# A four-graph pipelined graph network on one core: waits that name one graph, one order text for body, first and last group, and loads issued in the order's own turn

## What is computed

```
x = LN(x + (adj @ (x W + b)) / rowsum(adj))                       # layer 0
x = LN(x + softmax_i(q_i . (adj @ (k*mask))_i / 16) * (x Wv))     # layer 1, softmax over the nodes
x = LN(x + Wo(softmax(q k^T * 32^-0.5 * (adj + adj)) v) + bo)     # layer 2, 8 heads of 32
h = relu(D^-1 H B^-1 H^T (x W1^T) + b1);  h = LN(h)*gamma+beta    # layer 3, H = (adj != 0), 512 wide
x = LN(x + D^-1 H B^-1 H^T (h W2^T) + b2)
```

## Time and profile before

| | |
|---|---|
| median of 3 runs | 2016.6 us (2013.47 to 2019.37) |
| profiled execution, first to last instruction (span) | 2020.7 us |
| busy share PE / DVE / ACT / POOL | 94% / 85% / 72% / 62% |
| mean granted TensorE clock | 0.942 |
| HBM traffic | 46 MB, 23 GB/s on average |

### The profile page before, as it was taken

The page is one execution under the profiler, slowest core; times in us unless marked ns, Lnnn a source line. Parts: engine busy times, 40 slices in busy tenths (PEclk is TensorE's granted clock), DMA queues, the critical chain, the costliest instruction groups (busy, mean ns, idle before and its releaser), DMA issues.

```text
span 2020.7 us, 53237 instructions
## 1 busy us (share of the span) xinstructions
PE 1901.2 (94%) x15357; PEld 1690.6 (84%) x15357; DVE 1708.2 (85%) x4867; ACT 1456.1 (72%) x4431; POOL 1253.2 (62%) x2568
## 2 busy tenths in 40 slices
...
DMA packets 57546, 46.14 MB, mean 23 GB/s; under 512 B 5168, under 2 KB 56880, under 8 KB 57520
## 3 DMA queue, kind: packets, MB, share of 16 engines
...
## 4 chain that ended last, share of the span: by engine, by line
PE 73%; DVE 14%; issue 6%; ACT 5%; DVEq 1%; SPq 0%; DMA 0%; ACTq 0%; POOL 0%; POOLq 0%
PE ps L390 43%; PE ps L493 6%; PE ps L461 5%; DVE hb L872 3%; PE ps L482 3%; PE ps L406 3%; PE ps L453 3%; DVE z L894 3%; PE ps L469 3%; PE ps L442 2%; ACT z L629 2%; PE ps L374 2%; PE ps L427 1%; PE ps L400 1%; ACT x L573 1%
## 5 line engine op out<-in xcount | busy, mean ns | idle before, releaser
L629 ACT ACTIVATE z<-z,z_max 128x128 f32<-128x128 f32 x1024 | 401.5, 405 | 99.1 <-DVE z_max L905 99.0
L721 POOL TENSOR_TENSOR ln_rs<-ln_ve,minus_half 128x1 f32<-128x1 f32 x640 | 364.2, 569 | 50.1
L742 POOL TENSOR_TENSOR z<-z,z_rcp 128x1024 f32<-128x1024 f32 x128 | 242.7, 1896 | 226.3 <-DVE z_rcp L912 223.4
L719 POOL TENSOR_TENSOR ln_ve<-ln_mv,eps_col 128x1 f32<-128x1 f32 x640 | 128.4, 201 | 329.4 <-DVE ln_mv L791 329.1
L724 POOL TENSOR_SCALAR ln_nm<-ln_mv,ln_rs 128x1 f32<-128x1 f32 x640 | 170.7, 267 | 112.6 <-POOL ln_rs L721 112.6
L453 PE MATMUL ps<-kT,qT 32*128 32x128 f32 x2048 | 183.5, 323 | 57.7 <-DVE axT L801 29.8
L453 PEld LDWEIGHTS ps<-kT,qT 32*128 32x128 f32 x2048 | 137.0, 207 | 99.1 <-DVE axT L801 35.6
L894 DVE SCALAR_TENSOR_TENSOR z<-ps,a_hold 128x256 f32<-128x256 f32 x512 | 191.1, 416 | 34.1 <-PE ps L461 24.2
L390 PE MATMUL ps<-w2T,mnT 128*128 128x256 f32 x1536 | 208.6, 285 | 0.8 <-DVE mnT L801 0.7
L390 PE MATMUL ps<-w1T,txT 128*128 128x512 f32 x768 | 206.8, 404 | 0.1
L629 ACT ACTIVATION_READ_ACCUMULATOR z<-z,z_max 128x1 f32 x1024 | 206.6, 202 | 0.0
...
## 6 DMA issues: line engine op xcount, KB each, us to landing
x_in<-in_x_dram SPq DMA_DIRECT2D x32, 512.0 KB, 3.4
out_dram<-y_out SPq DMA_DIRECT2D x128, 128.0 KB, 1.7
a_in<-in_adj_dram SPq DMA_DIRECT2D x31, 256.0 KB, 2.7
x<-in_L_gnn_Wqk_dram ACTq DMA_DIRECT2D x1, 512.0 KB, 5.6
h<-in_L_gnn_W_dram SPq DMA_DIRECT2D x1, 512.0 KB, 5.2
h<-in_L_gnn_W_dram ACTq DMA_DIRECT2D x1, 512.0 KB, 10.6
v<-in_L_gnn_Wo_dram SPq DMA_DIRECT2D x1, 256.0 KB, 6.3
b_all<-in_L_gnn_b_dram SPq DMA_DIRECT2D x2, 128.0 KB, 8.3
```

The source lines that it names most:

```text
L629: m = act.activation(z[:, g % 2, h, :], z[:, g % 2, h, :], ACT.Exp, bias=z_max[:, g % 2, h:h + 1], accum_out=z_sum[:, g % 2, h:h + 1])
L719: pool.tensor_tensor(ve[n][:, g:g + 1], mv[n][:, g, 1:2], eps_col[:, :], ALU.add).then_inc(eps_made[n], 1)
L721: pool.tensor_tensor(rs[n][:, g:g + 1], ve[n][:, g:g + 1], minus_half[:, :], ALU.pow).then_inc(root_made[n], 1)
L742: pool.tensor_tensor(zg, zg, z_rcp[:, g % 2, :].unsqueeze(2).to_broadcast([P, HEADS, P]), ALU.mult)\
```

## The change

1. One text per engine, `ORDER_TEXT`, with `+` on the steps that are done for the next group and, on TensorE, the bank after a colon. `FIRST` and `LAST` are no longer written out: they are the steps with and without `+`, in the body's order and with the body's banks. The order and the banks of the body are the same as before.
2. Waits that free a buffer say which graph: `before(q, g, G)` in place of `q * G`, and `before(q, g, 2)` in place of `earlier(q, g, 2)`.
3. The waits on banks name the product that owned the bank (`bank_turns`), one wait for each owner.
4. Three waits are new: `am` on `made["amx"]`, and `dinv` on `read["h1"]` and `read["y"]`.
5. SP has a text as well: `lx.0+ la.0+ store.0 store.1 store.2 store.3`, walked like the others. The first `a_in` is now loaded by SP and not by ScalarE's queue.

```
-FIRST_TEXT = {
...
-LAST_TEXT = {
...
+    "sp": """
+        lx.0+ la.0+ store.0 store.1 store.2 store.3
+    """,
+FIRST = {engine: [s for s in schedule if s[2] == 1] for engine, schedule in ORDER.items()}
+LAST = {engine: [s for s in schedule if s[2] == 0] for engine, schedule in ORDER.items()}
...
-        def earlier(q, g, depth):
-            return q * G + (g - depth + 1) if g >= depth else q * G
+        def before(q, g, depth):
+            return q * G + (g + 1 - depth)
...
-            load_x(0)
-            load_x(1)
-            load_a(1)
-            with sp.Fori(0, NG - 2) as it:
-                load_x(it + 2)
-                load_a(it + 2)
-                store(it)
-            store(NG - 2)
-            store(NG - 1)
+            walk(FIRST["sp"], -1)
+            walk(ORDER["sp"], 0)
+            with sp.Fori(1, NG - 1) as it:
+                walk(ORDER["sp"], it)
+            walk(LAST["sp"], NG - 1)
...
             def walk(schedule, it, previous):
-                first, before = place_banks(schedule, previous)
...
+                for (stage, g, ahead, b), owners in zip(schedule, bank_turns(schedule, previous)):
+                    for other, og, away in owners:
+                        q = it + away
+                        pe.wait_ge(read[other], q + 1 if other in per_group else nth(q, og))
...
             def free1(q, g):
-                after(act, made["x1t"], q * G)
-                after(act, made["amx"], q * G)
-                after(act, norm_made["ln1"], q * G)
+                after(act, made["x1t"], before(q, g, G))
+                after(act, made["amx"], before(q, g, G))
+                after(act, norm_made["ln1"], before(q, g, G))
...
-            act.dma_start(a_in[:, :, :], adj_d[0:G].rearrange("g n m -> n g m")).then_inc(a_loaded, 16)
...
             def am(q, g, o):
                 dve.wait_ge(read["at"], nth(q, g))
                 dve.wait_ge(mask_made, q + 1)
+                after(dve, made["amx"], before(q, g, G))
...
             def dinv(q, g, o):
                 dve.wait_ge(read["mp"], nth(q, G - 1))
                 after(dve, x3c_made, q * G)
+                after(dve, read["h1"], q * G)
+                after(dve, read["y"], q * G)
```

More of the change, by code:

```diff
@@ L42 @@
     "pe": """
[L43 to L47, removed]
+        at.0+:0 sc1.0:1 ax.0+:3 at.1+:4 at.2+:5 sc0.0:6 ax.1+:0 sc1.1:1 sc0.1:3 at.3+:5 h0.0+:6 h0.1+:7
@@ new lines @@
+        ax.2+:0 mp.0:1 sc0.2:2 mp.1:4 mp.2:5 pt.0:6 h0.2+:0 ax.3+:1 mp.3:2 cx.0:3 sc1.2:4 pt.1:6 wo.0:0
+        x1t.0+:1 sc1.3:2 sc0.3:4 x1t.1+:6 cx.1:7 amx.0+:0 amx.1+:1 h0.3+:2 wo.1:3 tx.0:4 xg.0+:5 x1t.2+:6
+        xg.1+:7 amx.2+:0 pt.2:1 h1.0:3 x1t.3+:4 xg.2+:5 cx.2:6 tx.1:7 amx.3+:0 xg.3+:1 wo.2:2 pt.3:3 wt.0+:5
+        h1.1:6 cx.3:7 v1.0+:0 v1.1+:1 pb.0+:2 wo.3:3 tx.2:4 v1.2+:5 mn.0:6 h1.2:7 v1.3+:0 mn.1:1 x2t.0+:2
+        tx.3:3 y.0:4 h1.3:5 x2t.1+:6 y.1:7 mn.2:0 v2.0+:1 x2t.2+:2 v2.1+:3 x2t.3+:4 y.2:5 mn.3:6 k0.0+:7
@@ L48 @@
+        k1.0+:0 y.3:1 q1.0+:2 q0.0+:3 v2.2+:4 v2.3+:5
     """,
     "act": """
[L50 to L53, removed]
@@ L56 @@
+        relu.2 x2t.0+ tx.3 mn.1 ln1_norm.1+ ln3_norm.2 relu.3 x2t.1+ ln1_norm.2+ mn.2 ln1_norm.3+ x2t.2+
+        v2.0+ v2.1+ ln3_norm.3 x2t.3+ mn.3 ln4_norm.0 k0.0+ k1.0+ ln4_norm.1 q1.0+ ln4_norm.2 q0.0+ v2.2+
+        ln4_norm.3 v2.3+
     """,
     "dve": """
-        hyper.0 asum.0 sc1.0 zmax1.0 sc0.0 ax_lo.0 zmax0.0 sc1.1 ax_lo.1 zmax1.1 h0.0 zrcp.0 sc0.1 am.0 zmax0.1
-        ln0_stats.0 h0.1 ln0_aggr.0 am.1 ax_lo.2 am.2 ln0_stats.1 zrcp.1 sc0.2 zmax0.2 h0.2 ln0_aggr.1 ln0_stats.2
-        ax_lo.3 cx_lo.0 sc1.2 ln0_aggr.2 zmax1.2 wo.0 am.3 ln2_stats.0 sc1.3 x1t_lo.0 ln2_aggr.0 zmax1.3 sc0.3
@@ L61 @@
[L61 to L65, removed]
@@ L69 @@
     "pool": """
[L70 to L73, removed]
-    """,
-}
-FIRST_TEXT = {
[L78 to L97, removed]
@@ L128, with steps, bank_turns @@
 SPLIT = ("ax", "x1t", "x2t", "cx", "tx", "mn")
[L131 to L159, removed]
+def steps(text):
+    schedule = []
+    for word in text.split():
+        word, _, bank = word.partition(":")
+        stage, g = word.rstrip("+").split(".")
+        schedule.append((stage, int(g), 1 if word.endswith("+") else 0, int(bank) if bank else None))
+    return schedule
+ORDER = {engine: steps(text) for engine, text in ORDER_TEXT.items()}
+FIRST = {engine: [s for s in schedule if s[2] == 1] for engine, schedule in ORDER.items()}
+LAST = {engine: [s for s in schedule if s[2] == 0] for engine, schedule in ORDER.items()}
+BANK = {(stage, g): bank for stage, g, _, bank in ORDER["pe"]}
+def bank_turns(schedule, previous):
+    owner, turns = {}, []
+    for stage, g, ahead, bank in previous:
+        for b in range(bank, bank + BANKS[stage]):
+            owner[b] = (stage, g, ahead - 1)
+    for stage, g, ahead, bank in schedule:
+        mine = range(bank, bank + BANKS[stage])
+        turns.append(sorted({owner[b] for b in mine if b in owner}))
+        for b in mine:
+            owner[b] = (stage, g, ahead)
+    return turns
 def build(nc, ins, out):
@@ L336, in load_a, with store, walk @@
                 sp.dma_start(a_in[:, :, :], adj_d[bass.ds(q * G, G)].rearrange("g n m -> n g m")).then_inc(a_loaded, 16)
[L338 to L342 removed]
+            def store(q, g):
+                sp.wait_ge(norm_made["ln4"], nth(q, g))
+                sp.dma_start(out[bass.ds(q * G + g, 1)].rearrange("g n d -> n (g d)"),
+                             y_out[:, g, :]).then_inc(out_stored[g], 16)
+            stages = {"lx": load_x, "la": load_a, "store": store}
+            def walk(schedule, it):
+                for stage, g, ahead, _ in schedule:
+                    stages[stage](it + ahead, g)
             with nc.allow_non_contiguous_dma(reason="vectors, once"):
```

184 lines of the change are left out of this document (82 added, 102 removed).

## The result

The changed kernel takes 2179.0 us (median of 4 runs, 2177.6 to 2181.2) against 2015.0 us for the kernel before in the same comparison: a ratio of 1.082, 95% interval 1.080 to 1.084. It is 8% slower, 164 us by the medians and 156.8 us between the two profiled executions (2177.5 and 2020.7 us). The forecast was 2161 us, the range 2095 to 2222.

The account below looks back on a forecast made before the run. TensorE (PE), busy 94% of the span, was taken to bound the kernel. Seams 117 + clock 21 + registers 3 + first group 1 + last group 2 = 144 us on 2016.6 gave 2161 us, range 2095 to 2222.

Parts of the forecast that it names:

- SP's order costs, at 30 seams: Between turns, loads now issued behind the previous group's stores make everything 3.9 us later per seam, 117 us in all.
- The landing: At the seam, a_in lands at 927.5, 0.7 to 1.0 us after x_in; PE stands still 5.7 us before at.0.
- DVE's wait for a_in: Before the mask copy at each seam, DVE idles some 3 us in a wait that a DMA ends.
- The line of the Trainium skill: Fixed 2.0 us plus bytes over 436 GB/s: both loads in at 927.0, shift 3.4 us, sum 15 us less; not used.
- The shift behind the load and the clock: Per turn, 3.9 us later from the late load, plus 0.7 us for the lower clock (21 us in all).
- The clock's price: TensorE at its lower clock level: 6.8 us more there cost 2.7 us, so 0.4 us each.
- Narrower waits free nothing early: In the body, waits naming one graph are met long before they are asked: 0 us, bounds 0 and -19.
- Register work, 0.1 us per turn, 3 us: 6 more instructions each on ACT, DVE and POOL per turn, one or two on the seam's path; may be 0 or 7.
- First and last group, 1 + 2 us: Outside the turns, derived orders cost +1 us first (bounds -1, +4) and +2 us last (bounds -3, +8).
- the loads did not stay hidden: Rival: a_in lands before DVE comes to a_sum, so the seam costs nothing; 2004 to 2023 us, chance 0.03.
- the first rival: At the seam the load lands as if alone and the clock gives nothing: 2.7 us each, 2104 us, chance 0.14.
- The second: Rival: each standstill costs one more 6.8 us piece at the lower clock, 6.7 us per seam; 2221 us, chance 0.13.

Follow-up runs that it names:

- experiment 1: The changed kernel with SP's order alone undone, loads of group it+2 again ahead of the stores of group it: 2028.9 us, ratio 1.007.
- experiment 2: The kernel before with SP's order alone, loads of group it+1 behind the stores of group it-1: 2166.6 us, ratio 1.075.
- experiment 12: The kernel before with one wait more: POOL starts xb.0 at the head of a turn only when DVE's hyper.0 is done: 1919.6 us, ratio 0.954.
- experiment 4: The changed kernel with 21 matmuls of no use on PE ahead of at.0 in the loop: 2130.7 us, ratio 1.058.
- experiment 7: The kernel of experiment 1 with the buffer waits back on the previous group: 2010.3 us, ratio 0.996.
- experiment 6: The kernel before with only the derived first and last group, banks dealt as before: 2029.0 us, ratio 1.007.
- experiment 3: The changed kernel with SP's load of a_in ahead of that of x_in: 2147.2 us, ratio 1.066.

## Why the prediction was right

Step by step:

- *SP's order costs, at 30 seams.* Right, by experiments 1 and 2, one undoing it and one doing it alone: 150 and 150 us.
- *The landing.* Predicted: a_in in at 927.5 with ln4_norm.3 ending at 922.12, 5.4 us; measured 995.18 - 989.83 = 5.35 us. That it is so close is luck, since two errors of 0.4 us cancel. The loop's turn of SP took 0.58 us (990.33 to 990.91) where 0.2 was allowed. And the forecast counted the 3.4 us to x_in's landing from the end of its issue, where the page counts them from its start: 990.91 + 3.5 = 994.4, and POOL takes x_in up at 994.55, before 991.32 + 3.5 = 994.8. That a_in lands 0.7 to 1.0 us behind x_in was right: 991.56 + 3.6 = 995.16, 0.75 us behind. PE stands still 5.5 us; 5.7 was said.
- *DVE's wait for a_in* was said to be some 3 us and is 5.7 (172.0 / 30). The forecast took hyper.0 to be as slow as before; its four hb take 0.88 us at this seam and not 2.79, because POOL then stands waiting for x_in (experiment 12). The seam ends with a_in all the same, so the time doesn't show it.
- *The line of the Trainium skill* ("DMA: Bandwidth & Descriptors", section "Anatomy of one DMA", a fixed cost plus bytes) is given there for DMAs that GpSimd issues; these are SP's. By it the sum came out 15 us lower. From x_in's issue to a_in's landing the trace has 995.16 - 990.91 = 4.25 us where the line gives an estimated 3.8, and for a_in alone 2.7 against 2.6.
- *The shift behind the load and the clock.* Predicted 3.9 + 0.7 + 0.1 = 4.7 us per turn, measured 4.92. The split is less exact than the sum. Experiment 4, which takes most of the clock term away, leaves turns of 1948.4 / 30 = 64.95 us, 3.4 us above the kernel before, and puts 1.5 us on the lower clock, where 3.9 and 0.7 were said; but that kernel also has fewer falls than the one before had. That the fall comes before at.0 and at every seam was right, and that the old waits at the seam vanish.
- *The clock's price.* 0.4 us for each us at the lower level was read from two kinds of turn that differ in the dense stretch only. Experiment 4 gives 0.17 to 0.22 on average. It did no harm to the sum, since only a difference of some us per turn was priced with it, but experiment 4 came out 26 us above the near end of its expectation.
- *Narrower waits free nothing early.* Right. Experiment 7 has them as they were, and it is not slower.
- *Register work, 0.1 us per turn, 3 us.* Right in size. With early loads the short turns are 0.13 us longer than in the kernel before, registers and bank waits together. With late loads nothing of it is seen: the 12 us between the changed kernel and experiment 2 are the ends' 12. What the sum had no term for is that such a shift moves POOL against DVE: experiment 7 is 18.7 us faster than experiment 1 by one hb instruction per turn and the clock.
- *First and last group, 1 + 2 us.* Too small: 4.3 and 5.0 us between the profiles, 12 us by experiment 6. The first group's h0.3 stands behind amx.1 on PE: DVE evicts it at 42.09 us, where it was 37.26, and the layer norm of graph 3 with all that follows it is later for it. 4.3 us is beyond the bound of 4. These 6 us above the 3 said, with the 6.5 of the seams, are what the profile has above the 144 us predicted. The medians differ by 164 and not 157 because the profile of the kernel before, 2020.7 us, is 5.7 above its median of 2015.0, and that of the changed kernel, 2177.5, is 1.5 below its own.

The rivals: the loads did not stay hidden. Of the first rival, the landing as if alone is nearly what experiment 3 makes true; the forecast priced it at 30 x (3.9 - 2.7) = 36 us, and 32 are gained. Its other half, a clock that gives nothing, did not come. The second (one more piece of 6.8 us at the lower clock) came in the clock and not in its price: by the mean clocks the lower level went from 2 x 0.058 x 2020.7 = 234 to 392 us, 5 us more per turn, while the turns grew by 4.9 us and not by the 6.7 it named.
